# A stack of four gated attention and feed-forward layers: third attention in steps over three pairs, sliced loads, scaled rows in PSUM

## What is computed

```python
# per layer L: x = x + gate_a[L] * attn_L(norm(x));  x = x + gate_f[L] * ffn_L(norm(x))
# L0 attn : causal attention, 16 heads of 16, keys and values from ctx
# L0 ffn  : int8-like quantise/dequantise of rows and weights, silu(gate) * up, down
# L1 attn : y = Z + mean over time of (decayed scan of kv W_in) W_out; (y - mu)/sqrt(var) * gamma + beta
# L1 ffn  : eight 256x256 factors, summed, scaled by 1/sqrt(8), plus a bias
# L2 attn : scores = x ctx^T / 16, masked; softmax; readout = probs ctx; zero where nothing is valid
# L2 ffn  : 8 experts, top 2, plus a shared expert
# L3 attn : RMS-normalised queries and keys, 16 heads, masked by length; output projection
# L3 ffn  : 7 experts, top 2, plus one shared:
u = einsum('nh,ehi->eni', xt, Wup) + bup
g = silu(einsum('eni,eij->enj', u, Wgate) + bgate) * u
eo = einsum('enj,ejh->enh', g, Wdown) + bdown
```

## Time and profile before

| | us |
|---|---|
| median of three runs (lowest, highest) | 956.62 (954.14, 960.34) |
| profiled execution | 952.04 |
| its span | 950.2 |
| TensorE busy | 784.2 (83%) |
| VectorE busy | 609.7 (64%) |
| ScalarE busy | 422.2 (44%) |
| GpSimd busy | 356.2 (37%) |
| DMA queues moved | 116.98 MB |

### The profile page before, as it was taken

One profiled execution on the slowest core, in us unless ns is written; L12 is line 12 of the kernel. 1 busy time (PEld: TensorE's weight loads), 2 busy tenths in 40 slices (PEclk: granted clock), 3 DMA queues, 4 the chain that ended last, 5 costly groups with the idle time before them and its releaser, 6 DMA issues.

```text
span 950.2 us, 16486 instructions
## 1 busy us (share of the span) xinstructions
PE 784.2 (83%) x4525; PEld 504.5 (53%) x4525; DVE 609.7 (64%) x1445; ACT 422.2 (44%) x921; POOL 356.2 (37%) x619
## 2 busy tenths in 40 slices
PE   3939997887884188988989988899996989999980
PEld 2415554444442055667668856566664745666650
DVE  5729997678876967558232246488885776444445
ACT  3516665557771012323137747566664223333320
POOL 5000263345556523026837756100002583233330
PEclk9969999989995588555999997899999599999995
DMA  6461307999108880032535536100003122222217
GB/s 198 158 222 24 85 18 228 301 297 314 31 1 335 284 246 1 0 135 99 160 103 156 153 106 208 26 19 20 19 4 133 51 86 82 65 83 87 84 38 265
DMA packets 90650, 116.98 MB, mean 123 GB/s; under 512 B 12437, under 2 KB 81208, under 8 KB 89290
## 3 DMA queue, kind: packets, MB, share of 16 engines
q1 hardware_dynamic: 83802, 99.14, 34.2%
q0 software_dynamic: 6768, 16.86, 5.0%
HBM read 55.03 MB, written 58.43 MB: 119 GB/s over the span
## 4 chain that ended last, share of the span: by engine, by line
PE 53%; DVE 16%; issue 8%; SPq 6%; POOL 6%; ACT 6%; DMA 4%; DVEq 0%; ACTq 0%; POOLq 0%
PE ps L2153 9%; PE ps L2173 5%; PE ps L1739 4%; PE ps L1729 4%; PE ps L2044 4%; POOL x_rows L582 3%; SPq L386 3%; PE ps L1750 2%; PE ps L2062 2%; PE ps L1932 2%; PE ps L2002 2%; PE ps L2037 2%; PE ps L1775 2%; PE ps L2120 2%; PE ps L1949 2%
## 5 line engine op out<-in xcount | busy, mean ns | idle before, releaser
L812 ACT ACTIVATE probs_t<-ps 128x1024 f32<-128x1024 f32 x64 | 65.5, 1024 | 73.7 <-PE ps L1739 73.7
L1202 DVE TENSOR_REDUCE row_max<-ps 128x8 f32<-128x1024 f32 x64 | 77.8, 1215 | 19.2 <-PE ps L1729 17.2
L1208 DVE TENSOR_TENSOR work<-ps,row_max 128x1024 f32<-128x1024 f32 x64 | 77.5, 1211 | 2.3
L1596 DVE TENSOR_TENSOR ctx_cols<-ps,ctx_rows 128x512 f32<-128x512 f32 x54 | 37.3, 691 | 59.5 <-PE ps L2153 59.4
L1058 ACT ACTIVATE ctx_cols<-ctx_cols 128x256 f32<-128x256 f32 x54 | 22.5, 417 | 117.0 <-DVE ctx_cols L1596 111.6
L1739 PE MATMUL ps<-ident,work 128*128 128x128 f32 x512 | 70.0, 280 | 2.4 <-ACT work L806 2.1
L2153 PE MATMUL ps<-early,xt 128*128 x152 | 71.5, 593 | 0.0
L623 POOL DMA_INDIRECT y_rows<-ctx_cols,w2d x38 | 37.3, 981 | 81.5 <-DMA y_rows<-ctx_cols,w2d 45.2
L1739 PEld LDWEIGHTS ps<-ident,work 128*128 128x128 f32 x512 | 56.7, 142 | 17.4 <-ACT work L806 12.0
L2173 PE MATMUL ps<-early,ctx_cols 128*128 (+1 forms) x216 | 55.9, 381 | 5.6 <-ACT ctx_cols L1063 5.6
L2173 PEld LDWEIGHTS ps<-early,ctx_cols 128*128 128x128 f32 x216 | 40.6, 190 | 34.7 <-issue 24.6
(11 more groups left out here) (328 smaller groups left out, 1976.9 us busy)
## 6 DMA issues: line engine op xcount, KB each, us to landing
x_rows<-pad_row SPq DMA_DIRECT2D x1, 17415.0 KB, 67.6
work<-x_rows SPq DMA_DIRECT2D x77, 129.0 KB
x_rows<-pad_row SPq DMA_DIRECT2D x1, 7740.0 KB, 35.2
x_rows<-pad_row SPq DMA_DIRECT2D x1, 7611.0 KB, 92.8
early<-in_w3st SPq DMA_DIRECT2D x8, 512.0 KB
work<-y_rows SPq DMA_DIRECT2D x16, 256.0 KB, 2.9
early<-y_rows SPq DMA_DIRECT2D x8, 512.0 KB, 7.5
late<-in_w2u SPq DMA_DIRECT2D x1, 2304.0 KB, 10.2
```

Of the source, the lines that this page charges most:

```text
L812: act.activation(probs_t[:, :, :], ps[:, 4:6, :], ACT.Copy).then_inc(sem("att.evac"), 1)
L1202: dve.tensor_reduce(row_max[:, u, 8 * c:8 * c + 8], scores(c), AX.X, ALU.max).then_inc(sem("att.max"), 1)
L1208: dve.tensor_tensor(probs[:, u, c, :].rearrange("p (h k) -> p h k", k=P), scores(c), row_max[:, u, 8 * c:8 * c + 8].unsqueeze(2).to_broadc ...
L1596: dve.tensor_tensor(s3[:, i % 2], bank(i % 2), b_up[:, e], ALU.add).then_inc(sem("m3.sum"), 1)
```

## The change

Six edits are made together.

1. SP's loads are sliced between the stages of tiles 4 to 10. w_gu and w_dn come before tile 4, context 2 before tile 6, context 3 before tile 7, the transposed quantised weights before tile 8, the memory layer's loads before 9, mask and key weights before 10.
2. `keep_stats` is gone: the statistics go to `mv` directly.
3. `yg`, the scaled rows of the memory layer, are in PSUM banks 2 and 3.
4. VectorE's loops in the mixing, the third and the last attention are written out.
5. The third attention runs in ten steps. In step k TensorE does the front of pair k, the turn of k−2, the scores of k−1, the values of k−2, and in steps 1 to 8 half of one fused product; the rows have two buffers, and the two turned weights leave PSUM in one copy of 128x256.
6. So the first four fused products and their row sum leave the shared part. Their bank is 2 and their rows' 3; `product_out` runs in steps 3, 5, 7 and 9; `add_rows` stands at the head of the router's work on VectorE.

The diff, cut to its core:

```diff
-        yg = (o_n, tmp[:, 1])
...
+        xt4 = (xt, work[:, 5120:5632].rearrange("p (s j n) -> p s j n", s=2, j=2))
...
+        yg = [ps[:, 2 + i, :].rearrange("p (s d) -> p s d", s=2) for i in range(2)]
+
         def fuse_bank(e):
-            return 6 if e < EARLY else e - EARLY
+            return 2 if e < EARLY else e - EARLY
+
+        def fuse_rows(e):
+            return ps[0:E3 + 1, 3 if e < EARLY else 7, 0:D]
 
...
             stage_attention(sp, 0, 0, KR)
-            load_ctx(2)
-            load_ctx(3)
             sp.dma_start(wgu_raw, a["w_gu"].rearrange("(p o) d -> p o d", p=P)).then_inc(sem("load.ffn0"), 16)
             sp.dma_start(wdn_raw, a["w_dn"].rearrange("(p o) d -> p o d", p=P)).then_inc(sem("load.ffn0"), 16)
+            stage_attention(sp, 0, 4, 6)
+            load_ctx(2)
+            stage_attention(sp, 0, 6, 7)
+            load_ctx(3)
+            stage_attention(sp, 0, 7, 8)
             for dst, name in ((wgu_t, "wgu_t"), (wdn_t[0], "wdn_t0"), (wdn_t[1], "wdn_t1")):
                 sp.dma_start(dst, a[name]).then_inc(sem("load.wt"), 16)
+            stage_attention(sp, 0, 8, 9)
             sp.dma_start(bias_src[:, :], a["bias"]).then_inc(sem("load.bias"), 16)
             for dst, name in ((w_in, "w_in"), (w_out, "w_out"), (wsel, "wsel_c"), (b_in, "b_in"),
                               (b_out, "b_out"), (gam[:, :], "gam"), (bet[:, :], "bet")):
                 sp.dma_start(dst, a[name]).then_inc(sem("load.mem"), 16)
             sp.dma_start(kdec[:, 0:1], a["decay"]).then_inc(sem("load.mem"), 16)
+            stage_attention(sp, 0, 9, 10)
             sp.dma_start(mask_u8, a["mask"]).then_inc(sem("load.mask"), 16)
             for dst, name in ((w3kv, "w3kv"), (qk_c[:, 0:6], "qk_c")):
                 sp.dma_start(dst, a[name]).then_inc(sem("load.w3kv"), 16)
-
-            stage_attention(sp, 0, KR, NT)
+            stage_attention(sp, 0, 10, NT)
...
+            def evac_l2(k):
+                act.wait_ge(sem("l2.tr"), 2 * k + 2)
+                wait(act, sem("l2.pv"), 2 * k)
+                act.activation(pt_l2, bank(5, 2 * P).rearrange("p (s n) -> p s n", s=2), ACT.Copy).then_inc(sem("l2.evac"), 2)
+
+            def product_out(e):
+                upto(act, "wp.mm", e + 1)
+                act.activation(w13[:, e, :, D:2 * D], bank(fuse_bank(e)).rearrange("p (j n) -> p j n", j=2), ACT.Copy
+                               ).then_inc(sem("wp.out"), 1)
+
...
                     act.activation(p_l2[:, u], bank(u, P), ACT.Exp, scale=D ** -0.5, bias=sc_l2[:, u, 1:2],
...
+            for k in range(NT // 2 + 2):
+                if k < NT // 2:
+                    rows_l2(k)
+                if k >= 2:
+                    evac_l2(k - 2)
+                if 1 <= k <= NT // 2:
+                    exp_l2(k - 1)
+                if k >= 3 and k % 2 == 1:
+                    if k == 3:
+                        act.wait_ge(sem("kv.stored"), 32)
+                    product_out((k - 3) // 2)
...
-            def keep_stats(L, t):
-                dve.wait_ge(sem("bn.aggr"), NT * (L - 1) + t + 2)
-                dve.tensor_copy(mv[:, bass.ds(t, 2), :], mv2[:, :, :]).then_inc(sem("stats"), 2)
...
-                    dve.bn_aggr(mv2[:, u], st6[:, u]).then_inc(sem("bn.aggr"), 1)
-                keep_stats(L, t)
+                    dve.bn_aggr(mv[:, t + u, :], st6[:, u]).then_inc(sem("stats"), 1)
...
-                if A == 0:
-                    for t0 in range(0, NT, 2):
-                        body(t0, t0 == 0, t0 == NT - 2)
-                else:
-                    tile_pairs(dve, body)
+                for t0 in range(0, NT, 2):
+                    body(t0, t0 == 0, t0 == NT - 2)
...
-                if t:
-                    keep_stats(3, t - 2)
...
-            tile_pairs(dve, mixing)
...
+            for t in range(0, NT, 2):
+                mixing(t, t == 0, t == NT - 2)
...
-            tile_pairs(dve, attention2)
-            out_l2(NT - 2)
...
+            def out_l2(k):
...
+            for k in range(NT // 2 + 2):
+                if k + 1 < NT // 2:
+                    norm_x(4, 2 * k + 2)
+                if k >= 2:
+                    weights_l2(k - 2)
+                if 1 <= k <= NT // 2:
+                    maxima_l2(k - 1)
+                if k >= 2:
+                    out_l2(k - 2)
...
+            def add_rows(e):
+                upto(dve, "wp.mm", e + 1)
+                dve.tensor_tensor(brow[:, D:2 * D], fuse_rows(e), brow[:, D:2 * D], ALU.add).then_inc(sem("b3.row"), 1)
...
+            dve.wait_ge(sem("load.brow"), 32)
+            add_rows(EARLY - 1)
...
-                if i == 10:
-                    dve.wait_ge(sem("load.brow"), 32)
-                    add_rows(EARLY)
...
+            def fuse(e, halves=(0, 1)):
+                if 0 in halves:
...
+                    elif 0 < e < EARLY:
+                        upto(pe, "wp.out", e)
+                up_t, ga = wst[:, e % 4, 0], wst[:, e % 4, 1]
+                for c in halves:
+                    mm(fuse_rows(e), bupz[:, e, c, :], ga[:, c, :], start=(e in (0, EARLY) and c == 0),
+                       stop=(e in (EARLY - 1, E3) and c == 1), skip_group_check=True)
+                    for j in range(2):
+                        op = mm(ps[:, fuse_bank(e), c * D:(c + 1) * D], up_t[:, j, c * P:(c + 1) * P], ga[:, j, :], start=(j == 0),
+                                stop=(j == 1))
+                if 1 in halves:
+                    op.then_inc(sem("wp.mm"), 1)
...
+            for k in range(NT // 2 + 2):
+                if k < NT // 2:
+                    for u in range(2):
+                        front(4, 2 * k + u, u, lambda u: pe.wait_ge(sem("front.out"), FRONT[3] + NT))
+                if k >= 2:
+                    turn_l2(k - 2)
+                if 1 <= k <= NT // 2:
+                    scores_l2(k - 1)
+                if k >= 2:
+                    values_l2(k - 2)
+                if 1 <= k <= 2 * EARLY:
+                    fuse((k - 1) // 2, ((k - 1) % 2,))
...
+                    if L == 5 and t == 7:
+                        upto(pe, "wp.out", EARLY)
+                    elif L == 5 and t == 11:
+                        pe.wait_ge(sem("b3.row"), 1)
...
-                if 4 <= i < 4 + EARLY:
-                    fuse(i - 4)
```

More of the change, by code:

```diff
@@ L944, in attention2, with rows_l2 @@
                                    accum_out=sc_l2[:, u, 2:3]).then_inc(sem("l2.exped"), 1)
-            tile_pairs(act, attention2, peel=2)
-            evac_l2(NT - 2)
+            def rows_l2(k):
+                for u in range(2):
+                    act.wait_ge(sem("front.tr"), FRONT[4] + 2 * k + u + 1)
+                    wait(act, sem("main4"), 2 * k + u - 3)
+                    act.activation(xt4[k % 2][:, u], bank(TP + u, D).rearrange("p (j n) -> p j n", j=2),
+                                   ACT.Copy).then_inc(sem("front.out"), 1)
@@ L1425, in out_l2, with maxima_l2 @@
                                       ALU.mult).then_inc(sem("l2.gate"), 1)
+            def maxima_l2(k):
                 for u in range(2):
[L1427 to L1438 removed]
+                    dve.wait_ge(sem("main4"), 2 * k + u + 1)
@@ L1546, in _ @@
             hidden2(2)
-            def add_rows(n):
-                upto(dve, "wp.mm", n)
-                dve.tensor_tensor(brow[:, D:2 * D], ps[0:E3 + 1, 7, 0:D], brow[:, D:2 * D], ALU.add).then_inc(sem("b3.row"), 1)
             for i in range(NT + 2):
@@ L1582, in _ @@
             dve.wait_ge(sem("b3.row"), 1)
-            add_rows(E3 + 1)
+            add_rows(E3)
             for t in range(2, NT, 2):
@@ L1951, in attention2 @@
-            def attention2(t, first, last):
-                for u in range(2):
-                    front(4, t + u, u, lambda u: pe.wait_ge(sem("front.out"), FRONT[3] + NT))
-                if not first:
-                    attend_l2(t - 2, isinstance(t, int) and t == 2)
-                for u in range(2):
-                    pe.wait_ge(sem("front.out"), FRONT[4] + t + u + 1)
-                    wait(pe, sem("l2.exped"), t + u - 1)
-                    pe.wait_ge(sem("mask.add"), 1)
-                    mm(bank(u, P), ones3[0:1, :], mask_bf[0:1, t + u, :], start=True, stop=False)
-                    for j in range(2):
-                        op = mm(bank(u, P), xt[:, u, j, :], ctx_cols[:, t + u, j, :], start=False, stop=(j == 1))
-                    op.then_inc(sem("main4"), 1)
@@ new lines, in _, with turn_l2, scores_l2 @@
+            pe.wait_ge(sem("load.brow"), 32)
+            def turn_l2(k):
+                for u in range(2):
+                    pe.wait_ge(sem("l2.exped"), 2 * k + u + 1)
+                    if k == 0:
+                        pe.wait_ge(sem("resid3"), NT)
+                    wait(pe, sem("l2.evac"), 2 * k)
+                    pe.transpose(bank(5, (u + 1) * P, u * P), p_l2[:, u], ident[:, :]).then_inc(sem("l2.tr"), 1)
+            def scores_l2(k):
+                for u in range(2):
```

(20 more changed lines are left out.)

82 lines of the change are left out of this document (19 added, 63 removed).

## The result

The changed kernel takes 926.58 us (median of four runs, 926.32 to 928.05); the kernel before took 955.38 beside it. The ratio is 0.9693, with a 95% interval of 0.9654 to 0.9731: faster by 3.1%. The forecast was 922 in 909 to 936. The profiled execution took 928.05 us, its span 926.2. Against the profiled execution of before that is 24.0 less, where the sum said 32.3; the medians lie 28.8 apart. So the total hides errors, and they show stage by stage. The gain is what the stretch up to it added.

A forecast was written before the change was run, and what follows sets the result against it. No single engine was taken to bound the kernel; each stage had its own limit. Terms 14.5+2.8+5.3+1.5+1.5+6.7 = 32.3 us gave 919.7 against the profiled 952.04, or 924.3 as median; stated 922, range 909 to 936.

The forecast's parts named there:

- Loads sliced: First attention: stall before tile 4 falls from 16.4 to 0.2 us, partly lost again at tile 11; gain 14.5 us.
- tile 11 lands 99.5 to 101.5: First attention: tile 11's arrival after slicing, taken as 100.4, against 114.94 before; TensorE wants it at 96.
- The copy: Copy of the statistics removed from VectorE's chain: 2.0 us in the quantised layer, 0.8 in first attention, together 2.8.
- Scaled rows in PSUM: Memory layer: L1369 speeds up with one PSUM input, period 4.78 to about 4.05 us; gain 5.3 us.
- The 65 ns a read: Memory layer: estimated extra fixed cost of a VectorE PSUM read, 1 us for 16 reads; the forecast did not adopt it.
- Unrolled loops: VectorE's loops written out save idle and issue time: 1.5 us in the mixing, 1.5 in the last attention.
- Third attention: New steps at full clock, 5.2 and 6.4 us alternating, 45.3 in all where 52 stood; gain 6.7 us.
- the place of 366: Third attention: point in the earlier trace from which the forecast counted its new steps, beginning with a start of 3.8 us.
- The products leave the slot stage: First expert layer's shared part: GpSimd's 32 sends, not TensorE, set its end; gain 0, the first-slot wait grows.
- Rival A: Third attention: clock stays low; 945 us if wholly low, 930 to 940 for a part; chance 0.18.
- B: First attention: tile 11 takes back the slicing's gain, leaving 1 to 5 us instead of 14.5, 931 us; chance 0.07.
- C: Whole kernel: the changed kernel is slower than before; chance 0.03.

The follow-up runs named there:

- a4_exchange: Changed kernel with tile 11 staged before the two scale broadcasts and GpSimd's weight steps from tile 10 instead of 9: 919.0 us, ratio 0.9635 to the kernel before.
- a3_whole: Changed kernel with each late product's two row matmuls first, then its column groups, instead of alternating: 922.69 us, ratio 0.9676 to the kernel before.
- m2_noadd: Changed kernel with the scaled rows back in SBUF and GpSimd's beta additions cut to one element (beta left out of the output): 922.88 us, one run.
- c2_shared: Changed kernel with the first four products and row sum back in the first expert layer's shared part, new steps kept: 910.87 us, ratio 0.9541 to the kernel before.
- a2_copyout: Changed kernel with ScalarE's copy-out of a finished product ahead of the exponentials in the third attention: 921.83 us, ratio 0.9669 to the kernel before.
- n1_flat: Kernel before with the third attention's loops written out on TensorE, ScalarE and VectorE in the old order: 952.53 us, ratio 0.9988 to the kernel before.
- c5_values_first: c2_shared with the values before the next scores in each step of the third attention: 924.17 us, ratio 0.9661 to the kernel before.
- a1_block: Changed kernel with the four products in one block behind the third attention instead of halves in its steps: 927.48 us, ratio 0.9707 to the kernel before.

## Why the prediction was right, and where it was not

The direction and the range held. The sum gave 919.7 for the profiled execution and 928.05 came, 8.3 more; the median lies only 4.6 above the forecast, because 922 was set 2.3 above the sum.

- **Loads sliced** (14.5, measured 11.7). Tile 11's arrival came out within 0.7 us (101.05 for 100.4), SP's queue within 2. The step that was mis-sized is "tile 11 lands 99.5 to 101.5", taken as the whole cost: I had priced a half-speed restart behind the wait that goes and none behind the 5 us wait that comes. It cost 2.7. In the profiles of eight kernels with such a wait (4.8 to 5.5 us) the same two causal groups lie 5.0 to 6.4 apart, so it costs 1.5 to 2.9; in a4_exchange wait and cost are gone. The sum for SP's queue also leaves out the 1.2 us (36.99 to 38.16) of the two loads that stay in front of tile 4.
- **The copy** (2.8, of it 2.0 in the quantised layer, where 3.9 was measured): this term can't be read to 1 us. Two kernels with the same program up to there, the changed one and a3_whole, differ by 3.2 us in this layer (140.87 and 144.07 from the last causal group to the memory layer's first pair), with these stretches behind the first attention, of the changed kernel and of a3_whole:

```profile
147.40:159.40 12.00, 10.51 (x47) 4.95 (x48) 7.67 (x20) 3.89 (x7) 1.76 (x3) 0.86 1.09 311
```

```profile
148.10:160.10 12.00, 10.94 (x42) 4.94 (x44) 7.81 (x20) 3.49 (x5) 1.76 (x3) 0.72 1.09 304
```

Over all profiles the same stretch takes 142.3 to 147.7 in the five kernels with the copy and 139.4 to 144.1 in the nine without it; their means, 144.4 and 141.5, lie 2.9 apart, which bears out the sign of the term and roughly its size.

- **Scaled rows in PSUM** (5.3, measured 5.4): right in size and in mechanism. The 65 ns a read that I had worked out from the Trainium skill (VectorE: DVE Perf Modes, "The TRN2 errata — SBUF-src ops pay a fixed extra latency per instruction") don't show: a pair takes 0.87 us from PSUM and 0.88 from SBUF (m2_noadd).
- **Unrolled loops** (1.5 and 1.5, measured 0.6 and 0.5): the mixing period fell from 3.75 to 3.45, 1.8 in all, but two of its first products ran at half speed (2.08 and 2.05) where one had before. In the last attention the issue time before L1202's successor is gone, and the stage is hardly shorter: most of it had been covered.
- **Third attention** (6.7, measured 7.0): right in size by luck, through two errors that cancel. The steps were 0.5 to 0.6 shorter than forecast (4.71 and 5.77 for 5.2 and 6.4, and the wait for the copy-out 1.00 where I took 1.2), about 3 us in all, and the start was 3.5 longer (step 2 begins at 351.61; 3.8 behind the place of 366, which is 344.35 here, would be 348.1), because the clock fell at its head. The larger fault is that I set the whole against 52 and never worked out the steps without their halves. By my own terms that was 3.5 a step; c2_shared shows 3.7.
- **The products leave the slot stage** (0, measured 0.2): right, GpSimd's sends set the first slot. But the same passage says that they were free there, and the conclusion was not drawn: free work was moved to a place where it costs 10.5 us.
- **Not foreseen**, 4.1 us between the slots and the last attention and 1.3 at the end. The split late products are 1.2 of it. The rest is mostly two stretches at half speed that before did not have:

```profile
554.78 3.21 PE L2151 MATMUL ps<-xt,mid 128*128 128x256 f32 x8
...
749.09 3.34 PE L2184 MATMUL ps<-early,xt_all 128*128 128x512 f32 x4
```

The first is the queries' L2151, 3.21 for 1.89; the second an expert matmul group, 3.34 for 1.88. With the groups beside them they cost 1.7 and 1.6. The last slot waited 1.1 for VectorE, where it had waited 0.3. From the first slot to the last attention the changed kernel took 118.1 us, a2_copyout 118.2 and a4_exchange 118.4, but m2_noadd with the same instructions there 114.7; before it was 114.0, in c2_shared 114.3. So one program varies by 3.8 us there, and whether an edit makes the longer time more likely stays open.
- **Rival A**, the low clock, came true for 9 of 47 us. Rivals B and C did not: tile 11 took back 5 us, not the gain, and the longest of the 21 load issues took 1.02 us. The 0.03 of C stands for issues as long as the 3.43 of the earlier trace rows; no run shows what made those long.

## What to carry to other kernels

Before work is moved, ask whether it costs anything where it stands: four products were free beside a queue of sends, and moved onto the path of another stage they took back 10.5 of the 17.4 us that the new steps of that stage bring (54.1 us before, 36.7 without the halves, 47.2 with them). A wait of some us that a change creates has to be priced with the half-speed matmuls behind it, not by its length alone. And where an engine waits for another's copy inside a repeated step, put the next pair's independent work in between.

## What the runs showed of the hardware

- The order of a step can cost far more in clock than in waiting. With 0.24 us of waiting for the copy in a step of the third attention the clock was at 1.2 GHz for 43 us (n1_flat), with 0.52 for some 42 us in the profiled execution of c5_values_first; with the scores in the gap it rose to 2.4 GHz after the first steps and was there for nearly all of the rest (a1_block 0.95, c2_shared 0.94 from 352 to 378). What decides between the two was not measured further.
- Changing between matmuls of 8 and of 128 columns of weights costs TensorE: two halves take 3.17 us, the same twelve matmuls sorted by kind 2.88.
- A wait of 4.8 to 5.5 us before tile 11 brought a restart at half speed in eight kernels, worth 1.5 to 2.9 us; waits of 0.2 to 1.0 in the same stage brought none.
- A VectorE operation of 128x256 with two SBUF inputs took 867 ns beside GpSimd's additions of 800 ns on SBUF, 480 without them, and 473 beside them with one input in PSUM.
